# Two of every 32 exponentials of the third attention moved from ScalarE to VectorE

## What is computed

```python
def _L1_attn_b_ref(x):                       # B, T, D = 4, 1024, 128; 16 heads of hd = 8
    xh = x.reshape(B, T, H, hd)
    x_centered = xh - jnp.mean(xh, axis=1, keepdims=True)
    corr = jnp.einsum('bthd,bThd->bhtT', x_centered, x_centered)
    corr = jax.nn.softmax(corr, axis=-1)
    out = jnp.einsum('bhtT,bThd->bthd', corr, xh)
    return out.reshape(B, T, D)
```

## Time and profile before

| | |
|---|---|
| median of 3 runs | 3338.31 us (3337.55 to 3342.89) |
| the profiled execution | 3340.71 us, its span in the trace 3339.0 us |
| busy over the span: TensorE, VectorE, ScalarE | 2900.3, 2154.9, 2389.9 us |
| third attention, first to last exponential's start | 2786.8 to 3260.2 us |
| granted TensorE clock, mean of the span | 0.942 |

### The profile page before, as it was taken

One profiled execution on the slowest core, in us unless ns is written; L12 is line 12 of the kernel. 1 busy time (PEld: TensorE's weight loads), 2 busy tenths in 40 slices (PEclk: granted clock), 3 DMA queues, 4 the chain that ended last, 5 costly groups with the idle time before them and its releaser, 6 DMA issues. The chain is left out here.

```text
span 3339.0 us, 52935 instructions
## 1 busy us (share of the span) xinstructions
PE 2900.3 (87%) x17952; PEld 1300.8 (39%) x17952; DVE 2154.9 (65%) x3632; ACT 2389.9 (72%) x3588; POOL 210.8 (6%) x177
## 2 busy tenths in 40 slices
PE   4788888899999578988989999979979666999996
PEld 2221221566776311111147766632237551111115
DVE  6677777677676767777767767779999851000004
ACT  5689889555455679999955555556635557999994
POOL 2000000100000310000010000010000010000002
PEclk8899999999999789999989999989979867999997
DMA  4445443000000544444300000000000014232320
GB/s 113 71 62 69 65 68 47 26 0 0 0 0 1 133 84 62 66 56 64 53 31 0 0 0 0 0 27 1 1 1 0 2 38 86 46 52 49 52 49 28
DMA packets 76712, 125.47 MB, mean 38 GB/s; under 512 B 12937, under 2 KB 28201, under 8 KB 75629
## 3 DMA queue, kind: packets, MB, share of 16 engines
q1 hardware_dynamic: 76492, 122.65, 21.6%
HBM read 87.49 MB, written 29.16 MB: 35 GB/s over the span
## 5 line engine op out<-in xcount | busy, mean ns | idle before, releaser
L1845 ACT ACTIVATE m_mix_hidden<-m_mix_up_ps 128x512 f32<-128x512 f32 x512 | 305.7, 597 | 294.8 <-PE m_mix_up_ps L1761 294.8
L1079 ACT ACTIVATE b_direct_probs<-b_direct_s_ps 128x1024 f32<-128x1024 f32 x512 | 473.6, 1093 | 17.5 <-PE b_direct_o_ps L991 11.7
L1769 PE MATMUL m_mix_down_ps<-m_w,m_mix_hidden 128*128 128x128 f32 x4096 | 474.8, 276 | 0.0
L1079 ACT ACTIVATE c_att_probs<-c_att_s_ps 128x1024 f32<-128x1024 f32 x512 | 470.2, 1218 | 4.5 <-PE c_att_o_ps L991 3.0
L1769 PEld LDWEIGHTS m_mix_down_ps<-m_w,m_mix_hidden 128*128 128x128 f32 x4096 | 467.2, 192 | 15.3 <-issue 15.3
L1761 PE MATMUL m_mix_up_ps<-m_mix_ZT,m_w 128*128 128x512 f32 x1024 | 471.6, 618 | 0.0
L1079 ACT ACTIVATE a_direct_probs<-a_direct_s_ps 128x1024 f32<-128x1024 f32 (+10 forms) x512 | 431.8, 938 | 54.4 <-DVE a_direct_s_ps L1116 41.2
L1116 DVE SCALAR_TENSOR_TENSOR a_direct_s_ps<-distance,slopes,a_direct_s_ps 128x512 f32<-128x512 f32 (+3 forms) x512 | 355.3, 732 | 114.6 <-PE a_direct_s_ps L971 103.5
L1113 DVE TENSOR_TENSOR b_direct_s_ps<-b_direct_s_ps,distance 128x512 f32<-128x512 f32 x512 | 335.8, 695 | 142.4 <-PE b_direct_s_ps L971 141.5
L1102 DVE COPY c_att_taken<-c_att_o_ps 128x512 f32<-128x512 f32 x32 | 22.1, 692 | 453.5 <-PE c_att_o_ps L991 453.5
L991 PE MATMUL b_direct_o_ps<-b_direct_probs,v_cols 128*32 128x512 f32 x2048 | 275.1, 610 | 13.8 <-DVE b_direct_taken L1102 12.9
(11 more groups left out here) (375 smaller groups left out, 3365.4 us busy)
## 6 DMA issues: line engine op xcount, KB each, us to landing
qk_parts<-b_qkv_parts SPq DMA_DIRECT2D x48, 256.0 KB, 3.6
qk_parts<-a_qkv_parts SPq DMA_DIRECT2D x24, 256.0 KB, 3.4
a_k_rows<-qk_parts SPq DMA_DIRECT2D x32, 192.0 KB
a_q_rows<-qk_parts SPq DMA_DIRECT2D x32, 192.0 KB
b_k_rows<-qk_parts SPq DMA_DIRECT2D x32, 192.0 KB
b_q_rows<-qk_parts SPq DMA_DIRECT2D x32, 192.0 KB
qk_parts<-c_split_parts SPq DMA_DIRECT2D x24, 256.0 KB, 3.0
c_k_rows<-qk_parts SPq DMA_DIRECT2D x32, 192.0 KB
```

The source lines that it names most:

```text
L1079: act.activation(probs[:, J % 2, j, lo:hi], s_ps[:, slot(hg, n), lo:hi], ACT.Exp).then_inc(exped, 1)
L1769: last = pe.matmul(down_ps[:, t % 2, e, :], hidden[:, e * HALVES + h, t * P:(t + 1) * P], w["w2"][:, e * HALVES + h, :], start=(h == 0), s ...
L1845: act.activation(hidden[:, f, :], up_ps[:, f % UP_BANKS, :], ACT.Silu).then_inc(silu_done, 1)
```

## The change

In the third attention alone, `given = (31, 30)`: the exponentials of units 31 and 30 of each group are computed by VectorE. The units are processed in a new order: unit 31 is scored at place 2, unit 30 at place 15, the others keep their order in the remaining places. So units 0 and 1 are at places 0 and 1, units 2 to 13 at places 3 to 14, units 14 to 29 at places 16 to 31. Score buffers follow the place, `probs` and the order of the sums follow the unit. KEPT = 30 is the number of exponentials of ScalarE in a group.

For a given unit VectorE makes eleven steps on 128 x 1024: `take_power` (read the scores from PSUM, times log2 e, floor at -126, into `power`; this frees the score buffer), `round_power` (into int32 `whole`), and nine in `raise_two`: the rest, the exponent bits from `whole`, a polynomial of degree 6 in the rest, and the product, in `raised`. Each waits for the one that it depends on. Unit 31 of the next group is begun around the copies of this group's sums, unit 30 follows after them and after the reciprocals, if there are any. The last sum of a group, J = 7, reads `raised` for units 30 and 31 and waits for both.

```diff
--- before.py
+++ after.py
@@ -770,8 +770,13 @@
                         take_sum(QT - 1)
 
 
...
@@ -784,13 +789,21 @@
     NB = HG * UNITS
     SLOTS = 3
     TAKE_AT = (4, 7)
+    ORDER = [n for n in range(UNITS) if n not in given]
+    KEPT = len(ORDER)
+    NE = HG * KEPT
+    NG = len(given)
+    GIVEN_AT = (2, 15)[:NG]
+    for place, n in zip(GIVEN_AT, given):
+        ORDER.insert(place, n)
+    RAISE = 7
     LATER = 6
     INVERT_AT = (22, 26)
     SIDE = SEQ // 2
     span = span or (lambda h, J: (0, SEQ))
 
-    def slot(hg, n):
-        return (hg * UNITS + n) % SLOTS
+    def slot(hg, place):
+        return (hg * UNITS + place) % SLOTS
 
     def part(h, J, c):
 
...
@@ -887,7 +909,7 @@
 
             def ahead(b, hg):
 
-                sp.wait_ge(exped, b * NB + ((hg - 1) * UNITS + SLOTS + (LATER if hg == 1 else 0)))
+                sp.wait_ge(exped, b * NE + ((hg - 1) * KEPT + SLOTS + (LATER if hg == 1 else 0)))
                 operands.load(sp, hg % HG, b + hg // HG)
 
             def batch(b, first, final):
@@ -954,21 +976,25 @@
         def _(pe):
             pe.sem_inc(summed, 2)
 
-            def scores(hg, n, b):
-                J, j = divmod(n, GH)
+            def scores(hg, place, b):
+                J, j = divmod(ORDER[place], GH)
                 half = hg % 2
-                if n == 0:
+                if place == 0:
                     pe.wait_ge(loaded[half], b * (HG // 2 * operands.all_in) + (hg // 2 + 1) * operands.all_in)
-                at = hg * UNITS + n
+                at = hg * UNITS + place
                 back = at - SLOTS if at >= SLOTS else max(m for m in range(-SLOTS, 0) if slot(0, m + NB) == slot(0, at))
-                pe.wait_ge(exped, b * NB + (back + 1 + SLOTS))
+                of, was = divmod(back, UNITS)
+                if ORDER[was] in given:
+                    pe.wait_ge(powers_out, b * (NG * HG) + (of * NG + given.index(ORDER[was]) + 1))
+                else:
+                    pe.wait_ge(exped, b * NE + (of * KEPT + ORDER[was] + 1 + SLOTS))
                 for c in range(2):
                     if not part(hg * GH + j, J, c):
                         continue
                     left, right = part(hg * GH + j, J, c)
                     tile = int(c != J // (JT // 2)) if by_dve else c
                     rows = slice(PAIR_ROW * tile, PAIR_ROW * tile + operands.depth(tile))
-                    last = pe.matmul(s_ps[:, slot(hg, n), left:right], k_rows[rows, half, j, J * P:(J + 1) * P],
+                    last = pe.matmul(s_ps[:, slot(hg, place), left:right], k_rows[rows, half, j, J * P:(J + 1) * P],
                                      q_rows[rows, half, j, left:right], start=True, stop=True)
                 last.then_inc(scored, 1)
 
@@ -978,7 +1004,9 @@
                 if c == 0:
                     if J == 0:
                         pe.wait_ge(v_set, b * HG + (hg + 1))
-                    pe.wait_ge(exped, b * NB + (hg * UNITS + GH * (J + 1) + SLOTS))
+                    pe.wait_ge(exped, b * NE + (hg * KEPT + min(GH * (J + 1), KEPT) + SLOTS))
+                    if given and J == JT - 1:
+                        pe.wait_ge(raised_out, b * (NG * HG) + (hg + 1) * NG)
                 for j in range(GH):
                     h = hg * GH + j
                     meets = [i for i in range(JT) if part(h, i, c)]
@@ -988,8 +1016,10 @@
                     seen = part(h, J - 1, c)[1] if J > meets[0] else left
                     pieces = [(lo, hi) for lo, hi in ((left, min(seen, right)), (seen, right)) if lo < hi]
                     for lo, hi in pieces:
+                        n = J * GH + j
+                        weights = raised[:, given.index(n), lo:hi] if n in given else probs[:, J % 2, j, lo:hi]
                         last = pe.matmul(o_ps[VW * j:VW * (j + 1), c, lo - c * BANK:hi - c * BANK],
-                                         v_cols[:, hg % 2, J, j, :], probs[:, J % 2, j, lo:hi],
+                                         v_cols[:, hg % 2, J, j, :], weights,
                                          start=(J == meets[0]),
                                          stop=(J == meets[-1] and hi == right))
                 if c == 1:
...
@@ -1070,13 +1100,19 @@
 
             def batch(b):
                 for hg in range(HG):
-                    for n in range(UNITS):
+                    for place, n in enumerate(ORDER):
+                        if n in given:
+                            continue
                         J, j = divmod(n, GH)
                         lo, hi = span(hg * GH + j, J)
-                        act.wait_ge(adjusted if by_dve else scored, b * NB + (hg * UNITS + n + 1))
+                        if by_dve:
+                            act.wait_ge(adjusted, b * NE + (hg * KEPT + n + 1))
+                        else:
+                            act.wait_ge(scored, b * NB + (hg * UNITS + place + 1))
                         if j == 0:
                             act.wait_ge(summed, b * (HG * JT) + (hg * JT + J + 1))
-                        act.activation(probs[:, J % 2, j, lo:hi], s_ps[:, slot(hg, n), lo:hi], ACT.Exp).then_inc(exped, 1)
+                        act.activation(probs[:, J % 2, j, lo:hi], s_ps[:, slot(hg, place), lo:hi],
+                                       ACT.Exp).then_inc(exped, 1)
 
             with act.Fori(0, BATCH) as b:
                 batch(b)
@@ -1117,6 +1153,39 @@
                                                    op0=ALU.mult, op1=ALU.add)
                 ins.then_inc(adjusted, 1)
 
+            def take_power(b, hg, i):
+
+                dve.wait_ge(scored, b * NB + (hg * UNITS + GIVEN_AT[i] + 1))
+                dve.tensor_scalar(power[:, :], s_ps[:, slot(hg, GIVEN_AT[i]), :], LOG2_E, -126.0,
+                                  ALU.mult, ALU.max).then_inc(powers_out, 1)
+
+            def round_power(b, hg, i):
+                at = b * (NG * HG) + (hg * NG + i)
+                dve.wait_ge(powers_out, at + 1)
+                if hg or i or not isinstance(b, int) or b:
+                    dve.wait_ge(raised_out, at)
+                dve.tensor_copy(whole[:, :], power[:, :]).then_inc(rounded, 1)
+
+            def raise_two(b, hg, i):
+                at = b * (NG * HG) + (hg * NG + i)
+                done = b * (NG * HG * RAISE) + (hg * NG + i) * RAISE
+                rest, acc = power[:, :], raised[:, i, :]
+                dve.wait_ge(rounded, at + 1)
+                dve.tensor_tensor(rest, rest, whole[:, :], ALU.subtract).then_inc(stepped, 1)
+                dve.wait_ge(stepped, done + 1)
+                dve.tensor_scalar(whole[:, :], whole[:, :], 127.0, 8388608.0, ALU.add, ALU.mult).then_inc(doubled, 1)
+                dve.tensor_scalar(acc, rest, TWO_TO[6], TWO_TO[5], ALU.mult, ALU.add).then_inc(stepped, 1)
+                dve.wait_ge(stepped, done + 2)
+                dve.tensor_tensor(acc, acc, rest, ALU.mult).then_inc(stepped, 1)
+                for step in range(4):
+                    dve.wait_ge(stepped, done + (3 + step))
+                    dve.scalar_tensor_tensor(out=acc, in0=acc, scalar=TWO_TO[4 - step], in1=rest,
+                                             op0=ALU.add, op1=ALU.mult).then_inc(stepped, 1)
+                dve.wait_ge(stepped, done + 7)
+                dve.wait_ge(doubled, at + 1)
+                dve.scalar_tensor_tensor(out=acc, in0=acc, scalar=TWO_TO[0], in1=whole[:, :].bitcast(F32),
+                                         op0=ALU.add, op1=ALU.mult).then_inc(raised_out, 1)
+
             def invert(b, which, last=0):
                 n = (HEADS - last * GH) * HD
                 dve.wait_ge(gathered, b * 16 + 16)
@@ -1142,11 +1211,23 @@
                         if final and hg == HG - 1:
                             invert(b, 0, 1)
                             invert(b, 1, 1)
+                        following = given and not (final and hg == HG - 1)
+                        after = (b, hg + 1) if hg + 1 < HG else (b + 1, 0)
+                        if following:
+                            take_power(*after, 0)
                         take_sums(b, hg, 0)
+                        if following:
+                            round_power(*after, 0)
                         take_sums(b, hg, 1)
+                        if following:
+                            raise_two(*after, 0)
                         if hg == 1 and not first:
                             invert(b - 1, 0)
                             invert(b - 1, 1)
+                        for i in range(1, NG if following else 1):
+                            take_power(*after, i)
+                            round_power(*after, i)
+                            raise_two(*after, i)
                         continue
                     for n in range(UNITS):
                         adjust(b, hg, n)
@@ -1162,6 +1243,10 @@
                             if final and hg == HG - 1:
                                 invert(b, INVERT_AT.index(n), 1)
 
```

(7 more changed lines are left out.)

16 lines of the change are left out of this document (14 added, 2 removed).

## The result

The changed kernel takes 3382.92 us (median of 4 runs, 3377.26 to 3384.67), the kernel before 3340.6 (4 runs, 3337.55 to 3343.45) in the same comparison: ratio 1.0126 [1.0114, 1.0138], 42 us slower. The forecast was 3375 us, from a sum of 36 us more, with a range from 3356 to 3402: side and order of size were right, the loss is 6 us larger. The profiled execution took 3384.67 us, its span 3382.9, where before had 3340.71 and 3339.0.

The account below looks back on a forecast made before the run. ScalarE was taken to set the third attention's pace. Twelve groups at +2.1 us, three at +3.2 and the first at +1.4 made +36, giving 3377 by the profiled time or 3374 by the median; forecast 3375, range 3356 to 3402.

Parts of the forecast that it names:

- ScalarE's pace, and what is removed: Third attention: 0.917 us an exponential; two fewer a group cut ScalarE's floor by 1.83 us to 27.51, 29.3 over 16 groups.
- The order of TensorE: Third attention: sums waiting for later places stall ScalarE; with VectorE free a group takes 30.78 us, 1.44 more than now.
- The sums of J = 3 to 6: First-half sums waiting for place n+2 delay the next score pair: 0.65 us lost four times a group, 2.62.
- The wait of unit 0: At the group's end, next group's unit 0 waits for J = 6's second half to release its buffer: 0.30 us.
- Place 17: For J = 2, TensorE does sum, two pairs and second-half sum before place 17's pair: 0.35 us lost.
- J = 0 and 1 cost nothing: Sums of J = 0 and 1 wait only for place n+1; ScalarE has a scored place more, so no loss.
- VectorE late at place 15: take_power of place 15 comes only after unit 31's raise, delaying J = 3's sum: 0.64 us a group.
- The steps' prices: VectorE at 1024 columns: two inputs 1.22 us, one input or rounding 0.69, from PSUM 1.23; 12.1 us a given unit.
- The rival with slow int32 results: Two VectorE steps a unit with int32 results take 0.53 us more: 0.94 a group, 3389 us; chance 0.10.
- The clock: Rival: TensorE's idle time drops its clock to 1.2 GHz; 3387 us at three groups, 3407 in half; chance 0.11.
- a sign of being wrong: The forecast is wrong if J = 3 to 6 sums don't wait, two-input steps aren't 1.22 us, or clock leaves 1.00.
- The rival on the other side: TensorE's score pairs go while a sum waits, so ScalarE sets the pace: group 27.51, 3309 us; chance 0.09.

Follow-up runs that it names:

- the run with the moved wait: Kernel before, only the third attention's first-half sums of J = 0 to 6 waiting for two more exponentials: 3463.01 us, ratio 1.0374.

## Why the prediction was right, and where it fell short

- **ScalarE's pace, and what is removed.** Right: 480 exponentials, and with one given unit and only short stalls a group takes 28.65, where 31 x 0.917 is 28.43.
- **The order of TensorE: right mechanism, 0.26 too small a group.** Shown several ways: alone on the kernel before (a tile of 4.66 us), with VectorE's work taken away (31.03), and by moving the place (29.98) or places and sums together (28.28). Its terms can be read from the starts of ScalarE's runs in the kernel with the early `take_power`. The sums of J = 3 to 6 cost 0.68, 0.67, 0.66 and 0.67 us, 2.68 in all, for 2.62 forecast. The wait of unit 0 costs 0.32, for 0.30. Place 17 costs 0.51, for 0.35: this is the term that was mis-sized most. Its pair's 0.27 us of idle time was foreseen; the other 0.15 lies inside the run of 15 exponentials before it, 14.01 us long where 1.02 + 14 x 0.917 makes 13.86. It was put at nothing ("J = 0 and 1 cost nothing"), and the trace shows where it lies: at place 5, the fifth exponential of that run, which starts at 2943.39. TensorE made the second half of the group's last sum at 2945.70, the pair of place 5 only at 2946.70, and its exponential started at 2947.21, 1.07 after the one before and not 0.92. It is what the prediction had for place 17: the given place brings ScalarE nothing while TensorE makes a sum. The kernel with one given unit has the same 0.15.
- **VectorE late at place 15: right mechanism, 0.39 for 0.64.** Counted from the group's last first-half sum, at 2949.12, the pair of place 18 started at 15.02 (15.14 forecast) and the sum of J = 3 at 15.34 (15.41). Without the lateness, in the kernel with the early `take_power`, that sum started at 14.95, not 14.77. VectorE was as late as forecast, but TensorE's order was later than forecast, and covers more of it. The two errors cancel: 1.70 + 0.39 = 2.09 us a group, for 1.44 + 0.64 = 2.08.
- **The steps' prices.** Right: 1225 ns with two inputs, 689 and 695 with one, 1216 for `take_power`. The rival with slow int32 results is out: the rounding takes 689 ns. L1176 has a mean of 855 ns, but single ones 0.69, 0.77 beside GpSimd's copy and 2.84 beside its product. VectorE's busy time in the stage, 413 us by the groups, is 10 above the forecast, half of it from this line.
- **The sum: +36, measured +42.** In the stage of the profiled execution the loss is 39.6 (1.1 from the first group, 38.4 from the 15 periods that follow), to 1.4 and 34.8 forecast. Three periods are longer than forecast. The last is 35.02 us, for 31.4: GpSimd's product on VectorE's step, a wait that the sum put at nothing. The eighth, where the loop over batches begins anew, is 34.71 us; it had been 31.09, so the surplus over 2.1 is 1.5. It is 34.32 without VectorE's lateness too, so it is not VectorE's. The trace shows TensorE standing there, released by nothing that the profile shows:

```profile
3049.32 0.61 PE L997 MATMUL c_att_s_ps<-c_q_rows,c_k_rows 49*128 49x512 bf16 x4 [2.83 <-issue]
```

  It stood there for 2.04 us in the kernel before, and for 2.1 to 2.6 us in the traces of eight of the nine other runs. ScalarE's next exponential comes 2.9 us late, where the kernel before lost 1.8 in all; the slow stretch behind it (see the clock) costs 0.8 more, and VectorE's 0.4 is hidden in it: 1.5. Why TensorE stands there was not tried. The sixth is 33.60, with reciprocals, for 32.5; the other two with reciprocals took 32.31 and 32.24. Against these stand 1.7 us by which periods of before were themselves above 29.33 (or 31.09 for the eighth).
- **The clock.** Given 0.11 as a rival, it did fall, and the prediction had named that as a sign of being wrong; but it fell at three points, not in each group. In the windows of the changed kernel (columns as in the earlier trace rows):

```profile
2990.00:2995.00 5.00, 3.85 (x30) 0.71 (x26) 4.90 (x6) 4.74 (x6) 0.00 (x0) 1.00 0.34 58
2995.00:3000.00 5.00, 3.62 (x18) 0.59 (x22) 4.86 (x7) 2.03 (x3) 0.00 (x0) 0.66 0.04 13
...
3045.00:3050.00 5.00, 2.17 (x20) 0.55 (x22) 2.42 (x3) 2.19 (x3) 0.00 (x0) 1.00 0.03 7
3050.00:3055.00 5.00, 5.00 (x32) 0.63 (x26) 3.92 (x5) 4.21 (x5) 1.23 (x1) 0.66 0.04 8
...
3285.00:3290.00 5.00, 2.79 (x12) 0.44 (x14) 4.90 (x6) 1.14 (x2) 0.00 (x0) 0.63 0.00 0
3290.00:3295.00 5.00, 4.18 (x24) 0.49 (x20) 4.86 (x5) 3.85 (x4) 0.00 (x0) 0.69 0.00 0
```

These are the sixth, the eighth and the last period, the three that are too long. In each, TensorE had stood idle once for 2.01, 2.83 or 3.16 us before or in that stretch; a stretch at 0.63 to 0.69 is partly at 1.2 GHz and partly at 2.4. The ordinary waits of 1.2 us brought none. Nor does one wait's length decide: the two other groups with reciprocals had waits of 2.02 and 2.00 and kept 1.00, as did the kernel before behind its 2.04. That the falls make part of the surplus is read from these rows, not tried by itself.

The rival on the other side, that score pairs run ahead of a waiting sum, is refuted by the timeline at 2941.71 and by the run with the moved wait: TensorE took its instructions strictly in order.

## What to carry to other kernels

Moving work off the bound engine pays only if the order of the engine that feeds it still fits: here most of the loss came not from the work on VectorE, some 25 us a group, but from sums that stood two places too early in a queue that worked in order, with the next score pairs behind them. Most of the rest followed from one VectorE step that came too late. When units are reordered, renumber every hand-written order that counts them, and look at what is one place and what two places late: the first was free, the second cost 0.67 us each time. And a step that frees a buffer for others goes ahead of work that only its own engine needs; `take_power`, put one step of 1.22 us earlier, took 15 us off the time (3382.92 to 3367.85).
